# Prologue of a conditioned low-rank residual layer and a recurrence: loads, bias products and TensorE's order rearranged

## The reference, cut

```python
# layer 0, RANK = 8
c = layernorm(cond) * ln_gamma + ln_beta
h = gelu(c @ W1 + bias1)                      # [4, 256]
w = h @ W2 + bias2                            # [4, 8192]
a1, b1, a2, b2 = [t.reshape(B, D, R) for t in split(w, 4)]
u = einsum('btd,bdr->btr', x, a2)
mid = gelu(x @ base_down + einsum('btr,blr->btl', u, b2))
v = einsum('blr,btl->btr', b1, mid)
x = x + x + mid @ base_up.T + einsum('bkr,btr->btk', a1, v)
# layer 1
xW = x @ Wx + b
for t in range(512):
    h = tanh(xW[:, t] + h @ Wh)
    hs[:, t] = h
out = x + hs
```

## Time and profile before

| | |
|---|---|
| median of 3 runs | 527.63 us (527.47 to 527.81) |
| the profiled execution, its own time | 527.65 us |
| its span in the profile | 525.9 us |
| PE busy | 505.6 us, 96% |
| DVE, ACT, POOL busy | 291.8 us, 175.2 us, 22.2 us |
| first tanh of the recurrence (L462) starts | 38.02 us |

### The profile page before, as it was taken

One profiled execution on the slowest core, in us unless ns is written; L12 is line 12 of the kernel. 1 busy time (PEld: TensorE's weight loads), 2 busy tenths in 40 slices (PEclk: granted clock), 3 DMA queues, 4 the chain that ended last, 5 costly groups with the idle time before them and its releaser, 6 DMA issues.

```text
span 525.9 us, 33134 instructions
## 1 busy us (share of the span) xinstructions
PE 505.6 (96%) x14756; PEld 471.9 (90%) x14756; DVE 291.8 (55%) x2272; ACT 175.2 (33%) x1158; POOL 22.2 (4%) x35
## 2 busy tenths in 40 slices
PE   9999999999999999999999999999999999998885
PEld 6569999999999999999999999999999999998884
DVE  2535565565556556555655555555655655565553
ACT  3103333333333333333333333333333333333322
POOL 7350000000000000000000000000000000000000
PEclk9999999999999999999999999999999999999999
DMA  8970000000000000000000000000000000000000
GB/s 292 401 213 4 4 14 4 4 14 4 14 5 14 6 7 11 4 14 4 15 4 14 4 6 14 4 14 4 14 4 5 14 4 15 4 14 3 14 6 11
DMA packets 8114, 16.05 MB, mean 31 GB/s; under 512 B 500, under 2 KB 5924, under 8 KB 7972
## 3 DMA queue, kind: packets, MB, share of 16 engines
q1 hardware_dynamic: 7904, 13.90, 7.8%
q10 hardware_dynamic: 68, 0.05, 0.0%
HBM read 11.85 MB, written 2.10 MB: 27 GB/s over the span
## 4 chain that ended last, share of the span: by engine, by line
PE 94%; ACT 3%; issue 1%; DVE 1%; DVEq 0%; POOL 0%; POOLq 0%
PE bank L881 64%; PE bank L801 7%; PE bank L845 4%; PE bank L826 3%; ACT h_ring L462 3%; PE bank L850 2%; PE bank L840 2%; PE bank L821 2%; PE bank L831 2%; PE bank L648 2%; PE bank L682 2%; PE bank L810 1%; PE bank L661 1%; PE bank L785 1%; PE bank L869 1%
## 5 line engine op out<-in xcount | busy, mean ns | idle before, releaser
L881 PE MATMUL bank<-h_ring,whp 128*128 128x52 bf16 x6132 | 243.3, 186 | 13.2 <-ACT h_ring L462 13.2
L544 DVE TENSOR_TENSOR r_ring<-h_ring 128x4 f32<-128x4 f32 x1022 | 136.6, 164 | 205.7 <-ACT h_ring L462 203.2
L462 ACT ACTIVATE h_ring<-bank 128x4 f32<-128x4 f32 x1024 | 142.1, 174 | 320.3 <-PE bank L881 312.5
L881 PE MATMUL bank<-r_ring,whp 128*128 128x52 bf16 x4096 | 220.5, 185 | 0.0
L881 PEld LDWEIGHTS bank<-h_ring,whp 128*128 128x128 bf16 x6132 | 187.9, 96 | 34.2 <-ACT h_ring L462 25.8
L881 PEld LDWEIGHTS bank<-r_ring,whp 128*128 128x128 bf16 x4096 | 174.6, 96 | 0.0
L881 PE MATMUL bank<-l_ring,whp 128*128 128x52 bf16 (+1 forms) x2048 | 157.4, 178 | 0.0
L548 DVE TENSOR_TENSOR l_ring<-r_ring 128x4 bf16<-128x4 f32 x1024 | 136.2, 162 | 0.0
L881 PEld LDWEIGHTS bank<-l_ring,whp 128*128 128x128 bf16 x2048 | 122.5, 96 | 0.0
L801 PE MATMUL bank<-xp,wxp 128*128 128x32 bf16 x1488 | 63.0, 176 | 0.0
L801 PEld LDWEIGHTS bank<-xp,wxp 128*128 128x128 bf16 x1488 | 50.5, 96 | 0.0
(11 more groups left out here) (123 smaller groups left out, 240.4 us busy)
## 6 DMA issues: line engine op xcount, KB each, us to landing
w_sb<-in_L_cond_W SPq DMA_DIRECT2D x16, 512.0 KB, 11.5
out<-o_sb SPq DMA_DIRECT2D x16, 128.0 KB
x_sb<-in_x SPq DMA_DIRECT2D x3, 512.0 KB, 15.2
x_sb<-in_x SPq DMA_DIRECT2D x2, 256.0 KB, 9.6
w_sb<-in_L_cond_W SPq DMA_DIRECT2D x1, 256.0 KB, 3.6
down_sb<-in_L_cond_base_down SPq DMA_DIRECT2D x1, 256.0 KB, 5.0
wh_sb<-in_L_cond_Wh SPq DMA_DIRECT2D x1, 256.0 KB, 11.1
up_sb<-in_L_cond_base_up SPq DMA_DIRECT2D x1, 256.0 KB, 11.3
```

The costliest lines, as they stand in the source:

```text
L462: nc.scalar.activation(h_ring[:, m, slot(pair, s), 0:B], zt, ACT.Tanh).then_inc(h_ready, 1)
L544: nc.vector.tensor_tensor(r_ring[:, k, q, 0:B], state_before(pair, s, k)[:, 0:B], state_hi_before(pair, s, k)[:, 0:B], ALU.subtract).then_ ...
L881: return nc.tensor.matmul(zbank(p, q, m)[:, col0:col0 + n], whp[part][:, k, P * m:P * (m + 1)], rhs[:, 0:n], start=False, stop=stop, skip_ ...
```

## The change

**Loads.** W1 and the four transfers of A2 go first. The first 64 rows of x follow in four transfers, one for each batch, into `xa_sb` of 64 partitions by 4 rows of 256: each partition takes one 4-KB piece of four time rows, so a turned tile has its columns in the order (row of four, batch, quarter), and ACT's copy restores the order. Then base_down, Wh, B2, base_up, Wx, B1, A1. The other 64 rows of the first tile go into `xb_sb`, two batches side by side on the partitions. On ACT's queue bias2 moves from sixth to second.

**Bias products.** B1 and A1 get the upper half of the columns of the banks of A2 and B2, so that all eight bias products can stand before W2's products; those of B1 and A1 have `start=False`.

**PE's order.** See the rows below. ACT does the two gelus of `gT` before it copies x. The zero products go from 72 to 54.

```diff
-        PLACE = {A2: 0, B2: 2, B1: 0, A1: 2}
+        PLACE = {A2: (0, 0), B2: (2, 0), B1: (0, HC), A1: (2, HC)}
...
-            sp.dma_start(x_sb[0:T0, :, 0], x[:, 0:T0].rearrange("b p d -> p b d")).then_inc(ld_x[0], 16)
             sp.dma_start(w1_sb[:], W1.rearrange("(k p) n -> p k n", p=P)).then_inc(ld_w1, 16)
+            load_w2(A2)
+            for b in range(B):
+                sp.dma_start(xa_sb[T0 // 4 * b:T0 // 4 * (b + 1)], x[b, 0:T0].rearrange("(q r) d -> q r d", r=4)).then_inc(
+                    ld_xa, 16)
             sp.dma_start(down_sb[:], base_down.rearrange("(k p) n -> p k n", p=P)).then_inc(ld_down, 16)
-            load_w2(A2)
+            sp.dma_start(wh_sb[:], Wh.rearrange("(k p) n -> p k n", p=P)).then_inc(ld_wh, 16)
             load_w2(B2)
-            sp.dma_start(wh_sb[:], Wh.rearrange("(k p) n -> p k n", p=P)).then_inc(ld_wh, 16)
             sp.dma_start(up_sb[:], base_up.rearrange("(k p) n -> p k n", p=P)).then_inc(ld_up, 16)
+            sp.dma_start(wx_sb[:], Wx.rearrange("(k p) n -> p k n", p=P)).then_inc(ld_wx, 16)
             load_w2(B1)
-            sp.dma_start(wx_sb[:], Wx.rearrange("(k p) n -> p k n", p=P)).then_inc(ld_wx, 16)
             load_w2(A1)
-            sp.dma_start(x_sb[T0:P, :, 0], x[:, T0:P].rearrange("b p d -> p b d")).then_inc(ld_x_more, 16)
+            for b in range(B):
+                sp.dma_start(xb_sb[T0 * (b % 2):T0 * (b % 2 + 1), b // 2], x[b, T0:P]).then_inc(ld_xb, 16)
...
             act.dma_start(cond_sb[:], cond).then_inc(ld_cond, 16)
+            act.dma_start(bias2_sb[:], bias2.rearrange("(j c e n) -> e j c n", j=NTYPE, c=2, n=HC)).then_inc(ld_bias2, 16)
...
-            act.dma_start(bias2_sb[:], bias2.rearrange("(j c e n) -> e j c n", j=NTYPE, c=2, n=HC)).then_inc(ld_bias2, 16)
...
-                                 bias2_sb[:, j, c], start=True, stop=False, skip_group_check=True)
+                                 bias2_sb[:, j, c], start=(j in (A2, B2)), stop=False, skip_group_check=True)
...
+            pe.wait_ge(ld_bias2, 16)
+            pe.wait_ge(quadrant_ready, 1)
+            for j in (A2, B2):
+                for c in range(2):
+                    bias_product(j, c)
+            pe.wait_ge(cn_ready, 1)
...
-            w_products(B1, 1)
-            keep_busy(7, 7)
+            w_products(B1, 0)
...
-                    for b in range(2):
-                        e = 2 * k + b
-                        last = nc.tensor.transpose(more_rows_out(h)[:, T0 * e:T0 * (e + 1)],
-                                                   x_sb[T0:P, 2 * h + b, 0, P * k:P * (k + 1)], ident[T0:P, T0:P])
+                    last = nc.tensor.transpose(more_rows_out(h)[:, P * k:P * (k + 1)], xb_sb[:, h, P * k:P * (k + 1)],
+                                               ident[:])
```

More of the change, by code:

```diff
@@ L144, in adaptive_lowrank_then_recurrence @@
         ld_bias2 = sem("ld_bias2")
-        ld_x = [sem(f"ld_x{n}") for n in range(NTT)]
-        ld_x_more = sem("ld_x_more")
+        ld_xa = sem("ld_xa")
+        ld_xb = sem("ld_xb")
+        ld_x = [sem(f"ld_x{n}") for n in range(1, NTT)]
         ld_down = sem("ld_down")
@@ L414, in _ @@
                 nc.scalar.activation(gT[:, m, :], hpre(m), ACT.Gelu).then_inc(g_ready, 1)
+            for k in range(K2):
+                act.wait_ge(tr_ready, k + 1)
+                nc.scalar.copy(xT[:, k, :, 0:T0].rearrange("p b (q r) -> p r b q", r=4),
+                               bank[6 + k][:, 0:B * T0].rearrange("p (r b q) -> p r b q", r=4, b=B)).then_inc(tr_moved, 1)
             act.wait_ge(a2T_psum, 1)
@@ L645, in _, with keep_busy @@
             pe.wait_ge(pool_step, 1)
-            def keep_busy(n, spare=0):
+            def keep_busy(n, spare=4, first=False):
                 for _ in range(n):
-                    nc.tensor.matmul(bank[spare][:, D:2 * D], zeros_h[:, 0:P], zeros_h[:, 0:D], start=True, stop=True,
+                    nc.tensor.matmul(bank[spare][:, D:2 * D], zeros_h[:, 0:P], zeros_h[:, 0:D], start=first, stop=first,
                                      skip_group_check=True)
-            keep_busy(WARM)
+            keep_busy(WARM, first=True)
             pe.wait_ge(const_ready, 4)
@@ L667, in first_transposes @@
             def first_transposes(k):
-                for b in range(B):
-                    last = nc.tensor.transpose(bank[6 - k][:, T0 * b:T0 * (b + 1)], x_sb[0:T0, b, 0, P * k:P * (k + 1)],
-                                               ident[0:T0, 0:T0])
+                for r in range(4):
+                    last = nc.tensor.transpose(bank[6 + k][:, T0 * r:T0 * (r + 1)], xa_sb[:, r, P * k:P * (k + 1)],
+                                               ident[0:B * T0 // 4, 0:B * T0 // 4])
                 last.then_inc(tr_ready, 1)
@@ L676, in base_down_product, with w_half_products @@
                                  start=(k == 0), stop=False, skip_group_check=True)
+            def w_half_products(j, c, k):
+                pe.wait_ge(ld_w2[j][c][k], 16)
+                for e in range(NCH):
+                    last = nc.tensor.matmul(wbank(j, c)[Q * e:Q * (e + 1), :], gRep[:, k].rearrange("p b r -> p (b r)"),
+                                            w2_sb[:, k, j, HC * (NCH * c + e):HC * (NCH * c + e + 1)], start=False,
+                                            stop=(k == K2 - 1), skip_group_check=True)
+                if k == K2 - 1:
+                    last.then_inc(w_ready[j], 1)
             def w_products(j, c):
                 for k in range(K2):
[L680 to L686 removed]
+                    w_half_products(j, c, k)
             def turn_factor(j, done):
@@ L709, in a1_first_product @@
                                  stop=True, skip_group_check=True).then_inc(up_psum, 1)
-            pe.wait_ge(ld_x[0], 16)
-            first_transposes(0)
-            first_transposes(1)
-            keep_busy(4)
+            pe.wait_ge(ld_bias2, 16)
[4 more added lines that the diff above has]
+            pe.wait_ge(cn_ready, 1)
+            for k in range(K2):
+                last = nc.tensor.transpose(bank[5][:, D + B * k:D + B * (k + 1)], cn[:, P * k:P * (k + 1)],
+                                           ident[0:B, 0:B])
+            last.then_inc(cT_psum, 1)
+            bias_product(B1, 0)
             pe.wait_ge(ld_bias1, 16)
@@ L719, in _ @@
                                  start=True, stop=False, skip_group_check=True)
-            pe.wait_ge(cn_ready, 1)
-            for k in range(K2):
-                last = nc.tensor.transpose(bank[2][:, B * k:B * (k + 1)], cn[:, P * k:P * (k + 1)],
-                                           ident[0:B, 0:B])
-            last.then_inc(cT_psum, 1)
-            keep_busy(4)
-            pe.wait_ge(ld_down, 16)
-            base_down_product(0, 0)
             pe.wait_ge(ld_w1, 16)
@@ L769, in _ @@
                 keep_busy(4, 6)
-            w_products(B1, 0)
-            for c in range(2):
-                bias_product(A1, c)
             pe.wait_ge(upT_ready, 1)
```

87 lines of the change are left out of this document (43 added, 44 removed).

## The result

| | before | after |
|---|---|---|
| median | 527.57 us (527.15 to 527.81, 6 runs) | 532.52 us (529.92 to 535.11, 6 runs) |
| ratio to before, 95% interval | | 1.0099 [1.0067, 1.0131] |
| profiled execution, its span | 527.65, 525.9 us | 532.52, 530.6 us |
| first tanh of the recurrence starts | 38.02 us | 41.98 us |
| span less first tanh | 487.9 us | 488.6 us |

The change makes the kernel 1.0% slower; 525.2 was forecast, 524.4 to 527.0 the range. The after kernel's executions also lie further apart: 5.2 us from lowest to highest, before's 0.7.

What follows compares the result with a forecast made beforehand. TensorE's order, not the loads, was taken to bound the prologue; 2.1 us won there and 0.34 in the recurrence gave 527.65 - 2.1 - 0.34 = 525.2 us, range 524.4 to 527.0.

Steps and rivals of the forecast that it cites:

- the first part: Prologue up to W2's first products: they start at 11.40 us instead of 13.00, 1.60 won.
- The clock rises later: Rival, prologue: rise to 2.4 GHz at T costs (T - 6.2) / 2; T = 9.5 gives 526.9 us; chance 0.09.
- Slower, by the same place: Rival: 1.2 GHz holds through bias and first W2 products; 529.1 us at T = 14; slower for any reason 0.08.
- the gap is 0.7 of the 5 us: Argument against a later clock rise: TensorE idles only from 4.89 to 5.6 us.
- may be late by up to a microsecond: Layernorm's last step, behind gamma and beta: its possible delay is hidden by the four bias products until 7.8 us.
- bias2's landing: Start of the four bias products: bias2, issued earlier, lets them begin at 5.6 us, bounds 4.9 and 7.0.
- the 0.30 for the low clock: First bias products: 0.6 us of the four run at 1.2 GHz, which costs 0.30.
- The loads under the new order.: Prologue loads: A2 in by about 10 us, B2's last at 18.7 (wanted 18.78), A1's last 31.50 (wanted 33.0).
- The loads become the bound: Rival: x's four transfers cost 3.0 us more, B2's last lands at 21.7, kernel ends at 528.1; chance 0.05.
- Second to fourth part: Second u product to the first steps: 1.35 us won up to there, 1.3 at B1's turn, 2.1 at the recurrence.
- the 2.1 of the prologue: Start of the recurrence: the prologue's parts together win 2.1 us, first tanh near 36.
- In the recurrence: Two groups of four 64-row transposes become two full ones each: 0.34 us won, bounds 0 and 0.4.

Runs made afterwards that it cites:

- e1: The changed kernel with gamma and beta issued by SP ahead of W1 instead of by ACT: 530.91 us, ratio 1.008.
- e9: The changed kernel with gamma and beta on SP first, more zero products late in the prologue, bias2 on 100 rows (96 zeros): 528.56 us, ratio 1.0019.
- e10: e9 with x's first rows in one transfer of 1-KB rows, as before the change: 526.14 us, ratio 0.9985.
- e12: e10 with 256 KB of x written to 128 partitions instead of 64, so batches get wrong rows: 525.3 us, ratio 0.9965.
- e4: The changed kernel with more zero products around the prologue's last waits (9 for 5, 8 for 2, five more): 531.99 us, ratio 1.0097.
- e5: The changed kernel with all eight bias products made 128-row products of zeros, bias2 left out, beta still late: 527.08 us, ratio 1.0007.
- e3: The kernel before with only bias2 issued second on ACT's queue: 527.5 us, ratio 1.0015.
- e8: The changed kernel with gamma and beta on SP first, more late zeros, bias2 padded to 128 rows, its transfer waiting for the zeros: 536.35 us, ratio 1.0154.
- e6: The changed kernel with 128-row zero products as bias products (bias2 left out), gamma and beta on SP first, more late zeros: 526.07 us, ratio 0.998.
- e11: e10 with Wh issued behind B2, as in the kernel before: 526.0 us, ratio 0.9986.
- e7: The kernel before without its 12, 4 and 4 zero products up to W1's products: 529.88 us, ratio 1.0057.

## Why the prediction was wrong, point by point

**Where the 7.3 us between 525.2 and 532.5 lie.** In profiled executions the first tanh goes from 41.98 (after) to 38.36 when beta is on time (e1: 3.6, of which up to 1.7 is a shorter stretch at 1.2 GHz), to 36.7 to 37.3 when the bias products have 100 rows (e9, e10: 1.0 to 1.6), and to 35.80 when x goes to 128 partitions (e12: 0.9 to 1.5). That is 6.2 from 41.98 to 35.80. The 6.8 us at 1.2 GHz that e1 still has are worth up to 3.4; only 1.0 to 1.6 of it show in e9 and e10, in part because PE then waits for A2's or B2's last transfer and for x (0.3 to 0.7 each). The spans differ by 7.3 (530.6 and 523.3), so 1.1 lies behind the first tanh, 0.8 of it the second fall (e4).

**The step that failed: the sum of the first part.** It puts everything behind 6.2 us at 2.4 GHz, with 0.30 as the whole price of the clock, and has no wait at `cn`: 11.40. Measured was 15.30. The four bias products ended at 6.85, 1.0 sooner than in the sum; then came 1.78 of idle time; and from `cn` to W2's first product it took 6.66 instead of 3.56, 3.1 more, because the clock had fallen at 8.46. The sixteen W2 products behind took another 1.7 more.

The rivals "The clock rises later" and "Slower, by the same place" came nearest. They had 0.17 of the chances between them, but were priced for a late rise only; that a clock which is up could be lost in busy time has no term. The first was dismissed since "the gap is 0.7 of the 5 us", the second since "the trace of before shows no such long stretch at 1.2 GHz". But in before the bias products stood, one or two at a time, between products of 128 rows, so that its trace could not show what four in a row do. e1 shows the fall with no gap; e5 shows an execution without a fall and with a gap of 1.24; e9, with e1's early beta and real bias2 on 100 rows, shows none. The clock did rise on time (at 5.04, in the first bias product); it was lost at 8.46. The costs of the products themselves, at 2.4 GHz, were right: the four took 1.97 in e1, where 1.94 was forecast.

The Trainium skill (TensorE: Matmul & The Clock Gate, "What's actually happening" and "Why this matters for your kernels") lets the clock follow how busy TensorE has been recently, and its table of advice warns of idle gaps. Here the engine was busy without a gap and the clock fell (e1), so busy in the profile's sense was not enough; the number of rows at work mattered (4 in e1, 100 in e9).

**The term that was mis-sized: "may be late by up to a microsecond".** Beta was 3.0 late (7.62 against 4.60), and with it `cn` was ready 2.3 late (8.58 against 6.31). The forecast let the four bias products hide that until 7.8; they ended at 6.85, hid 0.5 of it and left 1.78 of idle time. 2.0 of the 3.0 come from bias2 alone (e3: 6.65); that the rest comes from A2's packets is argued from e8's 6.9, not shown separately.

**bias2's landing** (5.6 with bounds 4.9 to 7.0) came at 4.62; the bias products started at 4.75 with no wait. The 0.7 of idle time fell away, and of the 0.30 for the low clock 0.13 was left (2.10 against e1's 1.97), to the better.

**"The loads under the new order."** A2 "by about 10" was 10.34 in e1, 11.49 in after, and 11.9 to 12.5 in e5, e6 and e9 to e11, because the mean rate of 313 GB/s was used where 192 to 250 were moved between 9 and 12 us. B2's last came at 18.68, forecast 18.7, and A1's last at 31.73, forecast 31.50: both right in after, whose PE was too late to care. In e5, e6 and e9 to e11 B2's last was later, 19.3 to 21.2, and was waited for in e6 (1.36) and e10 (0.68). The rival "The loads become the bound" had this, but laid it on four small transfers; e10 refutes that, and e12 points to the partitions as the cause.

**Second to fourth part.** From the second u product to the first tanh after took 14.4, the forecast 14.2. In e12, with nothing of the failed steps left, the first tanh is at 35.80 (forecast near 36) and the time 525.07 in the profiled execution, 525.3 in the median: the 2.1 of the prologue can be had, with a load that isn't the reference's. That the end agrees is partly luck: W2's first product came at 10.58 (forecast 11.40) by the early bias2, and of these 0.8 won, 0.2 to 0.4 are left from the second `a1d` product (34.43, forecast 34.8) on.

**"In the recurrence", 0.34.** A step's group of transposes took 0.39 before and 0.28 in e12, so 0.22 for two steps, less than the 0.34 and within its bounds; by span less first tanh, 487.9 went to 487.3 to 487.5 in e9 to e12, 0.4 to 0.6. What makes up the rest was not looked into.

**Left open.** e10 and e11 are whole kernels, 0.15% faster by their medians with intervals that reach 1: not a proven gain. Two of the twelve of each lie at 528 to 531; none was profiled. Why the clock rose only at 23 or 24 us in e7 and e8, though full-row products ran long before, and what share an idle gap has in a fall, stays open too. x on 128 partitions with the right rows was not tried.

## What to carry to other kernels

Products that compute nothing, and full-row products between thin ones, may be holding TensorE's clock: before gathering thin products (few contraction rows) in one place, ask what else in that stretch uses all rows, and confirm the clock by durations. Put the few kilobytes that start a dependent chain ahead of everything on their queue and ahead of the big loads. Read the load rate from the stretch concerned, not from the mean, and look at how many partitions its transfers write.

## What the runs showed of the hardware that was not expected

- The fp32 products of 4 rows by 256 columns take as long as those of 128 rows (eight instructions, 1.97 and 1.99 us). In e1 a stretch of mostly the former lost 2.4 GHz at 8.13 without an idle gap; in the profiled e9 and e5, with 100 and 128 rows in their place, it was kept. Full rows did not bring a low clock up soon: in e8 it rose 13 us behind the start of 128-row products.
- A 4-KB transfer took 5.6 us behind 32 KB on its own queue and a large load on another; 32 KB issued 1.8 us later took 6.9 instead of 3.3 (e8).
- While x went to 64 partitions, all loads together ran at 192 to 264 GB/s (before: 204); with x on 128, at 371 (before: 339), with the DMA engines shown as fully busy in both.
- The clock's first rise differs between executions with the same work ahead of it: it came at 6.17 in before's profiled execution and at 3.72 in e3's, whose zeros up to there are the same (sixteen in 3.23 instead of 3.59). Before's runs on all chips spread from 526.2 to 528.1, after's from 529.9 to 535.1.
